# Two side banks and a ring of five, in place of one and six, in the sixteen-head context attentions

## The chip, the core and the metric

One core of a Trainium2 chip runs the kernel. Its engines work side by side: TensorE (PE in the profile, with PEld for its weight loads), VectorE (DVE), ScalarE (ACT), GpSimd (POOL), and the queue that issues transfers (SP). TensorE writes its results into PSUM, which the kernel holds as one tensor `PS` of 8 banks of 512 float32 numbers per partition; DVE and ACT read them from there. The metric is the device time of the kernel in microseconds (us): a median over runs.

## The reference, cut to what matters

The model is twelve sublayers on x, each added to x. Two of them, number 4 (`L1_xattn`) and number 10 (`L3_xattn`), are the ones that the change touches: cross attentions of 64 queries on 1601 context rows, in each of 16 batches, with 16 heads of 16.

```
def _L1_xattn_ref(q, k, v, Wq, bq, Wk, bk, Wv, bv, Wo, bo):   # q: (16, 64, 256); k = v = context: (16, 1601, 128)
    qh = (q @ Wq + bq).reshape(B, LQ, 16, 16).transpose(0, 2, 1, 3)
    kh = (k @ Wk + bk).reshape(B, LKV, 16, 16).transpose(0, 2, 1, 3)
    vh = (v @ Wv + bv).reshape(B, LKV, 16, 16).transpose(0, 2, 1, 3)
    scores = einsum('bhqd,bhkd->bhqk', qh, kh) / sqrt(16)
    attn = softmax(scores, axis=-1)
    out = einsum('bhqk,bhkd->bhqd', attn, vh)
    return out.transpose(0, 2, 1, 3).reshape(B, LQ, 256) @ Wo + bo
...
x = x + _L1_xattn_ref(_layernorm(x), ctx_512, ctx_512, ...)
...
x = x + _L3_xattn_ref(_layernorm(x), ctx_512, ...)            # the same without biases
```

## The kernel before, in words

`perceiver` runs the twelve sublayers one behind the other. `small_xattn` is the body of numbers 4 and 10: it normalizes x, makes the queries, and calls `head_attention` (L2037), the only function that changes. Number 4 (first = True) reads the context by rows, turns it with TensorE and stores the turned form; number 10 loads the turned form. Below they are the first and the second attention.

A batch has 13 tiles of up to 128 context rows (the last has 65). `head_attention` goes by cycles t. Batch and part of a cycle are t divided by 7 and its remainder, j, since a batch takes turns = 7 cycles of two key tiles (one in the last). 16 batches make t = 0 to 111, and before them stand 13 cycles that only prepare (t = -13 to -1). In cycle t TensorE does, in this order (L2292 to L2310):

- ST, `scores_turned(t)`, L2243 and L2252: scores with the keys on the partitions, shifted by the row maximum, into four banks of the ring (one for each group of heads);
- V, `values(t + 10)`, L2216: values of two key tiles, into the side bank;
- W, `weighted(t - 1, 0)`, L2272: half of the product of exps and values, into bank 7;
- S, `scores(t)`, L2231: scores with the queries on the partitions, of cycle t + 8's keys, into the next four banks of the ring, for the maximum alone;
- K, `keys(t + 12)`, L2206: turned keys, into the side bank;
- W, `weighted(t - 1, 1)`, L2272: the other half;
- at the end of a batch's j = 6 the turned row maximum (`max_turned`, L2282), at j = 5 the spread of the row sums (`sums_spread`, L2288), and in the first attention alone C, `context(t + 13)` (L2196), for four cycles of seven (j = 1 to 4; that of j = 4 has 65 columns); all three into the side bank.

Some parts are short: ST at j = 6, V at j = 3, S at j = 5, K at j = 1, and at j = 0 there is one W.

The other engines take these banks in the same order of cycles. ACT: the four exps of ST (`exps`, L2321), the keys (L2330), the sums, the context (L2349). DVE: the values (L2397, with a bias L2400), the four maxima of S (`block_max`, L2372), and once a batch the row maximum and the shift of it (`minus_max`, L2385), for which the next batch's ST waits.

What sets the order is this fixed list, with semaphores. Each fill of the ring has a number; it goes to the bank of that number modulo `banks`, and `wait_fill` lets TensorE wait until the fill with the number `banks` lower has been taken. Both ST and S call `wait_fill` for all four of their banks ahead of their first matmul. ST(t) has the numbers 8t + 32 to 8t + 35, S(t) 8t + 36 to 8t + 39 (for t from 0 to 103). Fills of the side bank are numbered too, and `wait_side` waits until the fill before has been taken.

Of the kernel before, what the change touches and what calls it, by code (L numbers as in the profile page):

```python
# [30 lines left out]
ACT = mybir.ActivationFunctionType  # L31
AX_X = mybir.AxisListType.X

P = 128
# [2002 lines left out]
def head_attention(core, room, Q, made, wv, biased, wo, wo_rows, oT, scale):  # L2037
# [21 lines left out]
    s_lead, v_lead, k_lead, c_lead = 8, 10, 12, 13  # L2059
    first, wk, pair_sel, sum_spread = room.first, made.wk, made.pair_sel, made.sum_spread  # L2060
    context_fills = -(-KT // 4)
    ring, banks, side, out_bank = 3, 6, 6, 7
    st_ready, exp_done = core.semaphore("scores_turned_ready"), core.semaphore("exps_ready")
    s_ready, max_done = core.semaphore("scores_ready"), core.semaphore("block_max_ready")
    top_ready, m_ready = core.semaphore("max_ready"), core.semaphore("shift_ready")
# [33 lines left out]
    for t in cycles:  # L2099
        due = []  # L2100
        if unit(t + v_lead) is not None:
            due.append(("values", t + v_lead))
        if unit(t + k_lead) is not None:
            due.append(("keys", t + k_lead))
        if (b := at_batch(t, turn_at)) is not None:
            due.append(("turn", b))
        if (b := at_batch(t, spread_at)) is not None:
            due.append(("spread", b))
        if (n := context_part(t)) is not None:
            due.append(("context", n))  # L2110
        for fill in due:
            fill_no[fill] = len(taken_by)
            count, by = (dve_no, side_dve) if fill[0] in ("values", "turn") else (act_no, side_act)
            count[fill] = len(count)
            taken_by.append((by, count[fill]))

    def st_fill(t):
        return 4 * (min(t + s_lead, total) + t)
# [16 lines left out]
    with ExitStack() as own:  # L2135
# [11 lines left out]
        with nc.Block() as block:  # L2147
# [29 lines left out]
            def _(pe):  # L2177
                def wait_side(fill):
                    n = fill_no[fill]
                    if n:  # L2180
                        by, count = taken_by[n - 1]
                        pe.wait_ge(by.sem, by.at(count + 1))

                def wait_context(b, to):
# [5 lines left out]
                def context(n):  # L2190
                    b, j = divmod(n, turns)
                    pe.wait_ge(room.landed[b % 2].sem, room.landed[b % 2].at(room.per_batch * (b // 2 + 1)))
                    wait_side(("context", n))
                    for k in range(4 * j, min(4 * j + 4, KT)):
                        kk = keys_of[k]
                        last = nc.tensor.transpose(PS[:, side, (k - 4 * j) * P:(k - 4 * j) * P + kk], room.rows[b % 2][0:kk, k, :],  # L2196
                                                   core.ident[0:kk, 0:kk])
                    last.then_inc(side_ready.sem, 1)

                def keys(t):  # L2200
                    b, u = divmod(t, turns)
                    lo, cols, chunks = key_cuts(u)
                    wait_context(b, lo)
                    wait_side(("keys", t))
                    for n, c in enumerate(chunks):
                        last = nc.tensor.matmul(PS[:, side, n * cols:(n + 1) * cols], wk[:, c * P:(c + 1) * P],  # L2206
                                                room.y[b % 2][:, lo:lo + cols], start=True, stop=True)
                    last.then_inc(side_ready.sem, 1)

                def values(t):  # L2210
                    b, j = divmod(t, turns)
                    wait_context(b, 256 * j)
                    wait_side(("values", t))
                    for n, kt in enumerate(tiles_of(j)):
                        kk = keys_of[kt]
                        last = nc.tensor.matmul(PS[0:kk, side, n * DIM:(n + 1) * DIM], room.y[b % 2][:, kt * P:kt * P + kk], wv[:],  # L2216
                                                start=True, stop=True)
                    last.then_inc(side_ready.sem, 1)

# [59 lines left out]
                def max_turned(b):  # L2279
                    pe.wait_ge(top_ready.sem, top_ready.at(b + 1))  # L2280
                    wait_side(("turn", b))
                    nc.tensor.transpose(PS[:, side, 0:P], M[:].rearrange("p i s -> p (i s)"),  # L2282
                                        core.ident[:]).then_inc(side_ready.sem, 1)

                def sums_spread(b):
                    pe.wait_ge(o_taken.sem, o_taken.at(b + 1))
                    wait_side(("spread", b))
                    nc.tensor.matmul(PS[:, side, 0:4 * SEQ], sum_spread[:], O[:, b % 2, :], start=True,  # L2288
                                     stop=True).then_inc(side_ready.sem, 1)

                pe.wait_ge(filled.sem, filled.at(4))
# [20 lines left out]
            @block.scalar  # L2312
            def _(act):
                def exps(t):
                    b, j = divmod(t, turns)
                    many, kk = len(tiles_of(j)), keys_of[2 * j]
                    if t >= ring:
                        act.wait_ge(av_done.sem, av_done.at(t - ring + 1))
                    act.wait_ge(st_ready.sem, st_ready.at(t + 1))
                    for i in range(groups):  # L2320
                        nc.scalar.activation(probs[0:kk, t % ring, i, 0:many].rearrange("p k c s -> p (k c s)"),  # L2321
                                             PS[0:kk, (st_fill(t) + i) % banks, 0:many * 2 * P], ACT.Exp,
                                             scale=scale).then_inc(exp_done.sem, 1)

                def keys_out(t):
                    b, u = divmod(t, turns)
                    lo, cols, chunks = key_cuts(u)
                    act.wait_ge(side_ready.sem, side_ready.at(fill_no["keys", t] + 1))
                    for n, c in enumerate(chunks):
                        last = nc.scalar.activation(kT[:, b % 2, c, lo:lo + cols], PS[:, side, n * cols:(n + 1) * cols], ACT.Identity)  # L2330
                    last.then_inc(side_act.sem, 1)

                def weighted_out(b):
                    act.wait_ge(av_done.sem, av_done.at((b + 1) * turns))
                    if b >= 2:
                        act.wait_ge(norm_done.sem, norm_done.at(b - 1))
                    nc.scalar.copy(O[:, b % 2, :], PS[:, out_bank, 0:4 * SEQ]).then_inc(o_taken.sem, 1)

                def sums_out(b):
                    act.wait_ge(side_ready.sem, side_ready.at(fill_no["spread", b] + 1))  # L2340
                    nc.scalar.copy(inverse[:, b % 2, :], PS[:, side, 0:4 * SEQ]).then_inc(side_act.sem, 1)

                def context_out(n):
                    b, j = divmod(n, turns)
                    cols = min(512, KEYS - 512 * j)
                    if j == 0 and b >= 2:
                        act.wait_ge(stored[b % 2].sem, stored[b % 2].at(16 * (b // 2)))
                    act.wait_ge(side_ready.sem, side_ready.at(fill_no["context", n] + 1))
                    nc.scalar.copy(room.y[b % 2][:, 512 * j:512 * j + cols], PS[:, side, 0:cols]).then_inc(side_act.sem, 1)  # L2349

                nc.scalar.activation(warm[:], core.ident[0:1, 0:1], ACT.Exp)
                for t in cycles:
                    if unit(t) is not None:
                        exps(t)
                    if unit(t + k_lead) is not None:
                        keys_out(t + k_lead)
                    if (b := at_batch(t, spread_at)) is not None:
                        sums_out(b)
                    if (n := context_part(t)) is not None:
                        context_out(n)  # L2360
                    if (b := at_batch(t, out_at)) is not None:
                        weighted_out(b)

            @block.vector
            def _(dve):
# [16 lines left out]
                def shift_rows(b):  # L2382
                    dve.wait_ge(side_ready.sem, side_ready.at(fill_no["turn", b] + 1))
                    for c in range(DC):
                        last = nc.vector.tensor_scalar(shift[:, b % 2, c, :], PS[:, side, 0:P], pair_sel[:, c:c + 1], None,  # L2385
                                                       ALU.mult).then_inc(m_ready.sem, 1)
                    dve.wait_ge(m_ready.sem, m_ready.at(2 * b + 2))
                    dve.sem_inc(side_dve.sem, 1)

                def values_out(t):  # L2390
                    b, j = divmod(t, turns)
                    kk, many = keys_of[2 * j], len(tiles_of(j))
                    dve.wait_ge(side_ready.sem, side_ready.at(fill_no["values", t] + 1))
                    bank = PS[0:kk, side, 0:many * DIM].rearrange("p (k h d) -> p k h d", h=heads, d=d)
                    out = V[0:kk, b % 2, 2 * j:2 * j + many, :, 0:d]
                    if not biased:
                        ins = nc.vector.tensor_copy(out, bank)  # L2397
# [736 lines left out]
```

## Time and profile before

| what | us |
|---|---|
| median of 3 runs (lowest to highest) | 5926.73 (5922.83 to 5929.96) |
| span of the profiled execution | 5928.5 |
| TensorE busy in the span | 5020.8 (85%) |
| DVE, ACT, GpSimd busy | 3277.9, 2125.8, 954.6 |
| first attention: first C to the first ST, first ST to that of t = 98 | 2032.7 to 2095.3, 2095.3 to 2698.6 |
| second attention: first K to the first ST | 4770.9 to 4821.7 |

The page gives no other time for the profiled execution than its span, which lies inside the range of the three runs; so spans are used as times. A row of the timeline is one group of like instructions in a row on one engine: its start, how long it lasted, and in brackets how long the engine sat idle before it, and whom it waited for. Starts of two groups subtracted give what a cycle costs; busy time alone does not, since pipelined matmuls overlap at their ends by about 0.07 us.

### The profile page before, as it was taken

How to read it: one execution, taken by the hardware profiler on the slowest of the kernel's cores; microseconds unless marked ns; L12 is line 12 of the kernel's file. 1: busy time of each engine (PE TensorE's matmuls, PEld its weight loads, DVE VectorE, ACT ScalarE, POOL GpSimd, SP SyncE). 2: the span in 40 equal slices, each digit the busy share in tenths (PEclk: the TensorE clock that was granted, in tenths of full speed). 3: DMA queues.
4: the chain of work that ended last, by engine and by line, in shares of the span. 5: the costliest groups of instructions: out<-in, count | busy, mean ns of one | idle time of the engine just before them, and what ended most of it. 6: DMA issues, size and time to landing. Idle time of an engine off the chain costs nothing. (4 is left out here: it accounts for less than half of the span.)

```text
span 5928.5 us, 114734 instructions
## 1 busy us (share of the span) xinstructions
PE 5020.8 (85%) x45710; PEld 3724.4 (63%) x45710; DVE 3277.9 (55%) x5626; ACT 2125.8 (36%) x3979; POOL 954.6 (16%) x423
## 2 busy tenths in 40 slices
PE   6879999987599899997756899986579989997877
PEld 4658888874489655555212788875159945555465
DVE  5367777762644455554699433354943355554453
ACT  1245555541155344443221333242024434443121
POOL 0022222100012000000365122142512200000200
PEclk8889999998599899999766899998779989999885
DMA  1010000001111111110010111033311010000020
GB/s 56 27 34 21 14 21 14 14 18 32 38 50 50 29 46 36 45 32 26 36 45 33 65 42 42 21 83 68 92 43 43 28 35 19 25 25 31 29 66 29
DMA packets 193278, 222.86 MB, mean 38 GB/s; under 512 B 44787, under 2 KB 166468, under 8 KB 184676
## 3 DMA queue, kind: packets, MB, share of 16 engines
q1 hardware_dynamic: 188772, 208.54, 11.3%
q10 hardware_dynamic: 4096, 8.40, 0.6%
q8 instruction: 313, 5.13, 0.4%
q14 instruction: 97, 0.79, 0.0%
HBM read 170.09 MB, written 15.34 MB: 31 GB/s over the span
## 5 line engine op out<-in xcount | busy, mean ns | idle before, releaser
L2372 DVE TENSOR_REDUCE block_max<-PS 128x1 f32<-128x512 f32 (+1 forms) x896 | 505.7, 628 | 203.6 <-PE PS L2231 203.6
L1632 PE MATMUL PS<-input_part,part_up 128*128 128x512 f32 x2304 | 552.1, 392 | 18.4 <-DVEq L1713 8.6
L1645 PEld LDWEIGHTS PS<-part_down,hidden_part 128*128 128x128 f32 x4608 | 548.6, 188 | 2.1
L1645 PE MATMUL PS<-part_down,hidden_part 128*128 128x256 f32 x4608 | 549.1, 281 | 0.0
L2321 ACT ACTIVATE probs_turned<-PS 128x512 f32<-128x512 f32 (+1 forms) x896 | 435.0, 571 | 314.6 <-PE PS L2252 314.6
L1632 PEld LDWEIGHTS PS<-input_part,part_up 128*128 128x128 f32 x2304 | 434.3, 189 | 110.3 <-DVEq L1713 9.3
L1685 ACT ACTIVATE hidden<-PS,b 128x512 f32<-128x512 f32 x384 | 265.0, 690 | 650.6 <-PE PS L1632 636.1
L844 PE MATMUL PS<-context_turned,queries 128*128 128x512 f32 x1728 | 411.9, 382 | 25.2 <-issue 18.5
L876 PE MATMUL PS<-probs_turned,context_part 128*128 128x256 f32 (+2 forms) x3120 | 409.2, 286 | 3.7 <-DVE weighted L953 3.7
L1721 DVE TENSOR_TENSOR hidden_part<-hidden,hidden_part 128x512 fp32r<-128x512 f32 x384 | 293.8, 774 | 182.9 <-ACT hidden_part L1675 182.1
L905 ACT CAST probs_turned<-PS 128x512 fp32r<-128x512 f32 x576 | 261.9, 511 | 358.6 <-PE PS L856 358.6
L876 PEld LDWEIGHTS PS<-probs_turned,context_part 128*128 128x128 f32 (+1 forms) x3120 | 382.7, 191 | 4.4 <-DVE probs_turned L919 4.3
L2630 POOL TENSOR_TENSOR fresh<-zT,b_all 128x1024 f32<-128x1024 f32 x64 | 214.4, 3350 | 988.7 <-DMA c_all<-bc_turned 850.7
L919 DVE TENSOR_TENSOR probs_turned<-PS,probs_turned 128x512 fp32r<-128x512 f32 x576 | 311.0, 582 | 97.4 <-ACT probs_turned L905 95.5
L844 PEld LDWEIGHTS PS<-context_turned,queries 128*128 128x128 f32 x1728 | 311.0, 196 | 85.7 <-issue 21.9
L2663 PE MATMUL PS<-prod,ident 128*128 128x512 f32 x256 | 208.4, 961 | 150.4 <-DVE prod L2649 150.4
L2272 PEld LDWEIGHTS PS<-probs_turned,values 128*17 128x17 f32 x13312 | 194.8, 97 | 189.6 <-issue 185.5
L911 ACT ACTIVATE probs<-PS,minus_max 128x1024 f32<-128x1024 f32 (+1 forms) x288 | 268.7, 935 | 87.6 <-DVE minus_max L964 86.7
L1552 POOL TENSOR_TENSOR part_up<-raw_up,part_up 128x2048 fp32r<-128x2048 f32 x24 | 110.4, 4600 | 1176.2 <-ACT part_up L1669 646.2
L1745 DVE SCALAR_TENSOR_TENSOR acc<-PS,gates,acc 128x256 f32<-128x256 f32 x192 | 92.2, 484 | 368.5 <-PE PS L1645 368.5
L959 DVE TENSOR_REDUCE row_max<-PS 128x1 f32<-128x1024 f32 (+1 forms) x288 | 272.7, 982 | 41.8 <-PE PS L844 41.3
L2644 DVE TENSOR_TENSOR_SCAN state<-decay,fresh 128x1024 f32<-128x1024 f32 x64 | 281.4, 4396 | 8.8 <-POOL fresh L2630 8.8
(427 smaller groups left out, 8391.6 us busy)
## 6 DMA issues: line engine op xcount, KB each, us to landing
context_rows<-in_ctx SPq DMA_DIRECT2D x40, 768.0 KB
raw_up<-in_L_ffn_W SPq DMA_DIRECT2D x16, 1024.0 KB, 4.8
raw_down<-in_L_ffn_W SPq DMA_DIRECT2D x16, 1024.0 KB, 4.8
ctx_turned<-context_turned SPq DMA_DIRECT2D x16, 800.5 KB, 4.8
context_turned<-ctx_turned SPq DMA_DIRECT2D x16, 800.5 KB
b_all<-bc_turned SPq DMA_DIRECT2D x16, 512.0 KB, 3.6
c_all<-bc_turned SPq DMA_DIRECT2D x16, 512.0 KB, 4.7
raw_up<-in_L_ffn_wg_w SPq DMA_DIRECT2D x8, 1024.0 KB, 4.8
```

Of the source, the lines that this page charges most:

```text
L844: last = nc.tensor.matmul(S[:, 512 * j:512 * j + cols], qs[a][:, v, p * P:(p + 1) * P], yT[b][:, v, 512 * j:512 * j + cols], start=(m == 0 ...
L876: last = nc.tensor.matmul(O_ps, yp[a][0:kk, u, k, :], probsT[b][0:kk, par, k, :], start=(k == 0 and m == 0), stop=(k == KT - 1 and m == 2))
L911: nc.scalar.activation(probs[:, local % 2, cols], S[:, cols], ACT.Exp, bias=bias[:, local % 2:local % 2 + 1], scale=scale, accum_out=total ...
L919: nc.vector.tensor_tensor(rest, bank, lead, ALU.subtract).then_inc(t_dve.sem, 1)
L959: nc.vector.tensor_reduce(top[:, q, half:half + 1], S[:, cols], AX_X, ALU.max).then_inc(step.sem, 1)
L1632: last = nc.tensor.matmul(PS[:, k % ring + 2 * x, :], bank.parts[name][a][:, c, f * P:(f + 1) * P], h[b][:, c, half * 512:(half + 1) * 512 ...
L1645: last = nc.tensor.matmul(PS[:, 4 + t % outs, 0:DIM], aT[a][:, f, t * P:(t + 1) * P], bank.parts["down"][b][:, f, :], start=(f == 0 and m ...
L1685: nc.scalar.activation(a32[:, k % depth, :], PS[:, k % ring, :], func, bias=b1s[:, bass.ds(e, 1), k % FC:k % FC + 1].squeeze(1)).then_inc( ...
L1721: nc.vector.tensor_tensor(hidden_part(1, k), a32[:, k % depth, :], hidden_part(0, k), ALU.subtract).then_inc(a_split.sem, 1)
L2321: nc.scalar.activation(probs[0:kk, t % ring, i, 0:many].rearrange("p k c s -> p (k c s)"), PS[0:kk, (st_fill(t) + i) % banks, 0:many * 2 * ...
L2372: nc.vector.tensor_reduce(part[:, b % 2, chunks[0]:chunks[-1] + 1, i, u // 2], bank, AX_X, ALU.max).then_inc(max_done.sem, 1)
L2644: nc.vector.tensor_tensor_scan(state[:, c % 2, :], decay[:, c % 2, :], fresh[:, c % 2, :], 0.0, ALU.mult, ALU.add).then_inc(h_ready.sem, 1)
```

## The change

`banks` goes from 6 to 5, and the single side bank (6) becomes two, banks 5 and 6, that the side fills take in turn. `wait_side` waits for the side fill two back instead of one back. `wait_fill` is unchanged in its text, but as `banks` is 5 it now waits for the fill five back. No instruction is added, removed or moved on any engine.

```
-    ring, banks, side, out_bank = 3, 6, 6, 7
+    ring, banks, sides, out_bank = 3, 5, 2, 7
...
+    def side_of(fill):
+        return PS[:, banks + fill_no[fill] % sides, :]
...
                 def wait_side(fill):
                     n = fill_no[fill]
-                    if n:
-                        by, count = taken_by[n - 1]
+                    if n >= sides:
+                        by, count = taken_by[n - sides]
                         pe.wait_ge(by.sem, by.at(count + 1))
...
-                        last = nc.tensor.matmul(PS[:, side, n * cols:(n + 1) * cols], wk[:, c * P:(c + 1) * P],
+                        last = nc.tensor.matmul(side_of(("keys", t))[:, n * cols:(n + 1) * cols], wk[:, c * P:(c + 1) * P],
                                                 room.y[b % 2][:, lo:lo + cols], start=True, stop=True)
...
-                    nc.tensor.transpose(PS[:, side, 0:P], M[:].rearrange("p i s -> p (i s)"),
+                    nc.tensor.transpose(side_of(("turn", b))[:, 0:P], M[:].rearrange("p i s -> p (i s)"),
...
-                    bank = PS[0:kk, side, 0:many * DIM].rearrange("p (k h d) -> p k h d", h=heads, d=d)
+                    bank = side_of(("values", t))[0:kk, 0:many * DIM].rearrange("p (k h d) -> p k h d", h=heads, d=d)
...
```

The lines left out put `side_of` in place of `PS[:, side, ...]` in the same way where the context, the values and the sums are written, and where ACT and DVE read them.

## Rows read from the trace of the kernel before

**Rows 1.** Timeline, TensorE, one batch of the second attention (start, us, engine, line)
```profile
5120.90 1.14 PE L2231 MATMUL PS<-keys_turned,queries 32*128 32x512 f32 x8
...
5123.60 0.50 PE L2243 MATMUL PS<-minus_max,ones_wide 32*128 32x512 f32 x4
...
5126.36 1.14 PE L2231 MATMUL PS<-keys_turned,queries 32*128 32x512 f32 x8 [0.22 <-ACT probs_turned L2321]
...
5137.68 0.67 PE L2231 MATMUL PS<-keys_turned,queries 32*128 32x65 f32 x16
...
5140.18 0.67 PE L2288 MATMUL PS<-weighted,sum_spread 128*128 128x256 f32 x2 [0.21 <-ACT keys_turned L2330]
5140.78 0.39 PE L2243 MATMUL PS<-minus_max,ones_wide 32*128 32x256 f32 x4
...
5147.44 0.50 PE L2243 MATMUL PS<-minus_max,ones_wide 32*128 32x512 f32 x4 [0.99 <-DVE minus_max L2385]
...
5150.40 1.14 PE L2231 MATMUL PS<-keys_turned,queries 32*128 32x512 f32 x8
...
5153.04 0.51 PE L2243 MATMUL PS<-minus_max,ones_wide 32*128 32x512 f32 x4 [0.45 <-DVE block_max L2372]
```

**Rows 2.** Line L2243: who its idle TensorE waited for (us, times)
```profile
  DVE block_max L2372: 24.4, 52
```

**Rows 3.** Timeline, DVE and ACT, the maxima and exps of one cycle
```profile
5151.60 1.29 DVE L2372 TENSOR_REDUCE block_max<-PS 128x1 f32<-128x512 f32 x2 [0.98 <-PE PS L2231]
...
5151.60 2.48 DVE L2372 TENSOR_REDUCE block_max<-PS 128x1 f32<-128x512 f32 x4 [0.98 <-PE PS L2231]
...
5154.56 1.09 ACT L2321 ACTIVATE probs_turned<-PS 128x512 f32<-128x512 f32 x2 [1.07 <-PE PS L2252]
...
5154.56 2.07 ACT L2321 ACTIVATE probs_turned<-PS 128x512 f32<-128x512 f32 x4 [1.07 <-PE PS L2252]
```

**Rows 4.** Timeline, TensorE, cycles with C in the first attention
```profile
2319.29 1.14 PE L2231 MATMUL PS<-keys_turned,queries 32*128 32x512 f32 x8
...
2322.11 0.51 PE L2243 MATMUL PS<-minus_max,ones_wide 32*128 32x512 f32 x4
...
2325.07 1.14 PE L2231 MATMUL PS<-keys_turned,queries 32*128 32x512 f32 x8
...
2328.04 0.63 PE L2196 MATMUL PS<-ident,context_rows 128*128 128x128 f32 x4 [0.21 <-ACT keys_turned L2330]
2328.60 0.51 PE L2243 MATMUL PS<-minus_max,ones_wide 32*128 32x512 f32 x4
...
2337.86 1.14 PE L2231 MATMUL PS<-keys_turned,queries 32*128 32x512 f32 x8
...
2341.07 0.50 PE L2243 MATMUL PS<-minus_max,ones_wide 32*128 32x512 f32 x4
```

**Rows 5.** Timeline, TensorE, the head of either attention
```profile
2067.51 1.14 PE L2231 MATMUL PS<-keys_turned,queries 32*128 32x512 f32 x8
...
2091.01 1.14 PE L2231 MATMUL PS<-keys_turned,queries 32*128 32x512 f32 x8
...
4773.18 2.04 PE L2206 MATMUL PS<-context_turned,wk 128*128 128x512 f32 x2 [0.78 <-ACT keys_turned L2330]
...
4798.71 1.14 PE L2231 MATMUL PS<-keys_turned,queries 32*128 32x512 f32 x8
...
4817.44 1.14 PE L2231 MATMUL PS<-keys_turned,queries 32*128 32x512 f32 x8
```

**Rows 6.** Timeline, TensorE, the tail of the first attention
```profile
2698.56 0.50 PE L2243 MATMUL PS<-minus_max,ones_wide 32*128 32x512 f32 x4 [0.98 <-DVE minus_max L2385]
...
2726.40 0.51 PE L2243 MATMUL PS<-minus_max,ones_wide 32*128 32x512 f32 x4 [0.92 <-DVE block_max L2372]
...
2739.76 0.51 PE L2243 MATMUL PS<-minus_max,ones_wide 32*128 32x512 f32 x4 [0.34 <-ACT probs_turned L2321]
```

**Rows 7.** Stretches: us, busy us of PE, PEld, DVE, ACT, POOL, PEclk, DMA
```profile
2094.00:2098.00 4.00, 3.01 (x38) 2.51 (x39) 1.22 (x4) 0.34 (x1) 0.00 (x0) 0.69 0.00 0
...
2725.00:2730.00 5.00, 3.30 (x134) 2.81 (x130) 2.57 (x5) 2.07 (x4) 0.00 (x0) 1.00 0.02 3
...
5120.00:5280.00 160.00, 150.69 (x2985) 90.77 (x2987) 90.78 (x157) 71.80 (x151) 0.00 (x0) 1.00 0.07 23
```

More of the change, by code:

```diff
@@ L2195, in context @@
                         kk = keys_of[k]
-                        last = nc.tensor.transpose(PS[:, side, (k - 4 * j) * P:(k - 4 * j) * P + kk], room.rows[b % 2][0:kk, k, :],
+                        last = nc.tensor.transpose(side_of(("context", n))[:, (k - 4 * j) * P:(k - 4 * j) * P + kk], room.rows[b % 2][0:kk, k, :],
                                                    core.ident[0:kk, 0:kk])
@@ L2215, in values @@
                         kk = keys_of[kt]
-                        last = nc.tensor.matmul(PS[0:kk, side, n * DIM:(n + 1) * DIM], room.y[b % 2][:, kt * P:kt * P + kk], wv[:],
+                        last = nc.tensor.matmul(side_of(("values", t))[0:kk, n * DIM:(n + 1) * DIM], room.y[b % 2][:, kt * P:kt * P + kk], wv[:],
                                                 start=True, stop=True)
@@ L2287, in sums_spread @@
                     wait_side(("spread", b))
-                    nc.tensor.matmul(PS[:, side, 0:4 * SEQ], sum_spread[:], O[:, b % 2, :], start=True,
+                    nc.tensor.matmul(side_of(("spread", b))[:, 0:4 * SEQ], sum_spread[:], O[:, b % 2, :], start=True,
                                      stop=True).then_inc(side_ready.sem, 1)
@@ L2329, in keys_out @@
                     for n, c in enumerate(chunks):
-                        last = nc.scalar.activation(kT[:, b % 2, c, lo:lo + cols], PS[:, side, n * cols:(n + 1) * cols], ACT.Identity)
+                        last = nc.scalar.activation(kT[:, b % 2, c, lo:lo + cols], side_of(("keys", t))[:, n * cols:(n + 1) * cols], ACT.Identity)
                     last.then_inc(side_act.sem, 1)
@@ L2340, in sums_out @@
                     act.wait_ge(side_ready.sem, side_ready.at(fill_no["spread", b] + 1))
-                    nc.scalar.copy(inverse[:, b % 2, :], PS[:, side, 0:4 * SEQ]).then_inc(side_act.sem, 1)
+                    nc.scalar.copy(inverse[:, b % 2, :], side_of(("spread", b))[:, 0:4 * SEQ]).then_inc(side_act.sem, 1)
                 def context_out(n):
@@ L2348, in context_out @@
                     act.wait_ge(side_ready.sem, side_ready.at(fill_no["context", n] + 1))
-                    nc.scalar.copy(room.y[b % 2][:, 512 * j:512 * j + cols], PS[:, side, 0:cols]).then_inc(side_act.sem, 1)
+                    nc.scalar.copy(room.y[b % 2][:, 512 * j:512 * j + cols], side_of(("context", n))[:, 0:cols]).then_inc(side_act.sem, 1)
                 nc.scalar.activation(warm[:], core.ident[0:1, 0:1], ACT.Exp)
@@ L2384, in shift_rows @@
                     for c in range(DC):
-                        last = nc.vector.tensor_scalar(shift[:, b % 2, c, :], PS[:, side, 0:P], pair_sel[:, c:c + 1], None,
+                        last = nc.vector.tensor_scalar(shift[:, b % 2, c, :], side_of(("turn", b))[:, 0:P], pair_sel[:, c:c + 1], None,
                                                        ALU.mult).then_inc(m_ready.sem, 1)
```

## The prediction

> **What bounds the kernel now.** I first read the stretches, to see which engine sets the pace where the change acts. In the second attention TensorE is busy 150.69 of 160 us at a granted clock of 1.00 (2.4 GHz), DVE 90.78 and ACT 71.80 [rows 7]. So TensorE nearly sets the pace, with some 6% idle. Then I read TensorE's own timeline over one batch, for what ends that idle time. There are four kinds of wait: for the maxima (0.45 us at 5153.04), for the exps (0.22 us at 5126.36), for `minus_max` at the start of each batch (0.99 us at 5147.44), and for the single side bank (0.21 us at 5140.18, behind the keys) [rows 1]. The first two are waits of the ring, the last is the wait that the change is about. Line L2243 waits for the maxima 52 times, 24.4 us in all [rows 2]: the ring of six is already just too small in those cycles, and just large enough in the others.
>
> The two time spans that decide are from one ST to the S behind it, and from that S to the next ST.
>
> **What a ring of five waits for.** ST(t) begins at number F = 8t + 32. With six banks its four fills wait for F-6 to F-3: the last exps of ST(t-1), and the first two maxima of S(t-1). With five they wait for F-5 to F-2: one exp and the first three maxima. In the same way S(t) waits today for the last two maxima of S(t-1) and the first two exps of ST(t); with five banks for the first three exps. All waits stand ahead of the first matmul. So each ST waits for one maximum more, each S for one exp more.
>
> One maximum more is (2.48 - 1.29)/2 = 0.60 us later, one exp more (2.07 - 1.09)/2 = 0.49 us later [rows 3].
>
> Where the ring is the limit today the spans can be read: S to ST by the maxima takes 5153.04 - 5150.40 = 2.64, ST to S by the exps 5126.36 - 5123.60 = 2.76 [rows 1]. With the change these bounds become 2.64 + 0.60 = 3.24 and 2.76 + 0.49 = 3.25, and nothing that TensorE has to do in between is that long, except with C. One cycle then lasts 6.49 us. These are rows of this kernel with one step of this kernel added, so I take them at their value. Below them the cost could be nothing, if the engines were ahead of TensorE by a maximum; the waits of 0.45 and 0.22 exclude that. Above them, a wake-up could be paid once more: 0.15 us lie between the end of the second maximum (5151.60 + 1.29) and ST at 5153.04 [rows 1, 3], and 0.15 at some 12 waits a batch in 28 batches is 50 us more, 6066. I take the value without it, since that 0.15 is already inside 2.64 and 2.76.
>
> **The second attention, batch by batch.** ST to S: 2.96 where V is whole (5150.40 - 5147.44 [rows 1]; j = 0, 1, 2, 4, 5), becomes 3.25: five times +0.29. At j = 3 (V short) +0.49. At j = 6 ST is short, its exps are done in time: no change. Together +1.94. S to ST: +0.60 at j = 0 and j = 1, where the maxima decide already. At j = 2, 3, 4 it is 2.70 (5123.60 - 5120.90 [rows 1]) and becomes 3.24: three times +0.54. At j = 5 S is short and its maxima are no limit; the wait of the sums' spread for the keys goes, 0.21 and the 0.05 of overlap that a wait costs, -0.26. At j = 6 the next ST waits for `minus_max`, which stands on DVE behind all four maxima: what is gained for the turned maximum is hidden by them, no change. Together 1.20 + 1.62 - 0.26 = +2.56. A batch costs +4.50. For t = 0 to 97, 14 batches: **+63.0 us**.
>
> **The first attention.** ST to S as before, +1.94. S to ST holds C at j = 1 to 4. At j = 1 it is 2.82 (2322.11 - 2319.29) and becomes 3.24, +0.42. At j = 2 and 3 it is 3.53 (2328.60 - 2325.07), of which 0.26 is C's wait for the keys [rows 4]; that goes, 3.27 is left, and the maxima's 3.24 lie below it: twice -0.26. At j = 4 3.21 (2341.07 - 2337.86 [rows 4]) becomes 3.24, +0.03. At j = 0 +0.60, at j = 5 -0.26. Together +0.27, a batch +2.21. 14 batches: **+30.9 us**. Here the change gets some of its gain, and C's work covers part of the new wait.
>
> **The tails.** From t = 98 on no C and soon no K is left. The five cycles from 2698.56 to 2726.40 take 27.84 [rows 6] and become 5 x 6.49 = 32.45: +4.6. Then one exp step +0.5, and five cycles in which ST alone waits for the exps (0.34 us at 2739.76 [rows 6]), each +0.49: +2.4. Two tails of +7.5: **+15.0 us**.
>
> **The heads.** In the cycles without ST the side bank is the limit: V waits for the keys, K for the values, at 0.78 us each (as at 4773.18 [rows 5]). This goes, and the maxima's bound takes its place where S runs: S to S 3.24. Second attention: the five cycles from 4798.71 to 4817.44 take 18.73 [rows 5]; four of them become 3.27, the one behind the short S 2.8 (V, S and K by TensorE's own time), 15.9: -2.8. Before 4798.71, six fills run at 1.2 GHz one behind the other instead of with 0.78 to 0.88 us between them; if the clock rises at the same moment as today, that leaves -4.3. First attention: from 2067.51 to 2091.01 23.50 [rows 5] becomes 16.5 (C, V, S and K without waits: 3.3, 3.3, 3.8, 3.4, 2.8): -7.0, and before it -5.1. Together **-19.2 us**. An earlier rise of the clock would give up to 5 us more in each head; a fall of it at the end of the head, as at 2094 [rows 7], costs some 2 us now and may or may not come.
>
> **The sum**: 63.0 + 30.9 + 15.0 - 19.2 = +89.7 on a span of 5928.5, 6018. The span lies 1.8 us above the median, so the forecast is 5926.7 + 89.7 = **6016 us**, 1.5% slower.
>
> The Trainium skill ("Perfetto Trace Analysis", Optimization Strategy) says that the same gap repeating on the engine that should be saturated can mean too little PSUM for the next tile. By it the gaps at C, the spread and the turned maximum speak for a second side bank, but those at L2243 speak for the ring, which is larger in count; the trace agrees with the rule for both.
>
> **Rivals.**
>
> A. The gain of the side banks shows and the ring has slack enough (faster). Its place: all waits for the side bank, its price the heads' -19.2, -0.26 for three cycles of a first-attention batch and one of a second, 14 x 1.04 = -14.6; together -34, 5893 us. It decides if a third maximum is taken by the time that ST comes. Against it: at 5153.04 ST waits already for the second [rows 1].
>
> B. The clock. With 6.49 us cycles TensorE has some 0.8 us idle in each, in two pieces. At 2094 the granted clock fell to 0.69 for 4 us, after a head with gaps in each cycle [rows 7]. If it fell like that at each of 32 batch starts, at 2 us each, the time would be 64 us more, 6080. Against it: from 2725 to 2730 TensorE is busy 3.30 of 5 us, with longer gaps than the change makes, at clock 1.00 [rows 7]. The Trainium skill ("TensorE: Matmul & The Clock Gate", A second HAM failure mode: psum-queue depth-cycling) describes just this, small idle times between groups that cycle through banks making the clock swing. By the rule rival B would hold; no row of the main loop shows it.
>
> C. The new waits cost less than I count, half of 0.29 and 0.54, because TensorE's own groups could slip behind one another or maxima start earlier: 93.9 + 15.0 halved, minus 19.2, is +35, 5962 us. For it nothing speaks but that small waits have hidden slack; against it, that both bounds are read from waits.
>
> D. The ring and the side banks balance, within 0.2% (12 us, about what a measurement of this kernel can tell from no change): it needs a third of the ring's cost and all of the heads' gain.
>
> **Chances.** The forecast, from 5995 to 6040: 0.78. B 0.07. C 0.07. D 0.03. A 0.04; 0.01 for the rest. The range that holds the time 8 times in 10 reaches down for the heads' clock and part of C and up for the wake-ups: 5988 to 6045. Slower 0.93, same 0.03, faster 0.04.
>
> **What would show it.** Right: on L2243 the waits for the maxima grow from 24.4 us to above 100 us, and stand in front of nearly every ST of the second attention; on L2231 waits for the exps appear in six cycles of seven, about 0.3 us each; a batch of the second attention lasts 45.2 us instead of 40.7, one of the first 45.3 instead of 43.1; L2196, L2282, L2288, L2216 and L2206 wait for no keys or values. The first ST stands about 12 us and 7 us earlier behind the start of its attention. Wrong: batches as long as today, or a granted clock below 1.00 between the batches.

## The result and the profile after

The changed kernel takes 5996.46 us (median of four runs, 5994.20 to 6003.85), the kernel before 5924.79 us beside it (5922.83 to 5929.96). The ratio is 1.0121, with a 95% interval from 1.0107 to 1.0136: slower by 71.7 us where 89.7 were forecast. The forecast was 6016 us with a range from 5988 to 6045; the result lies inside it, 19.5 us below the forecast. The profiled span grew from 5928.5 to 5994.3 us, by 65.8; the account below is one of the spans.

The code stands three lines further down in the changed kernel: ST is L2246 and L2255, S L2234, V L2219, K L2209, C L2199, W L2275, the turned maximum L2285, the maxima L2375, the exps L2324.

First the page of the changed kernel. DVE and ACT do what they did; what changed is when TensorE may write.

```profile
PE 5013.0 (84%) x45710; PEld 3726.0 (62%) x45710; DVE 3276.2 (55%) x5626; ACT 2123.5 (35%) x3979; POOL 955.5 (16%) x423
```

The same 160 us of the second attention as in [rows 7], with the same columns, and who line L2246 waited for (us, times), as in [rows 2]:

```profile
5120.00:5280.00 160.00, 137.64 (x2698) 83.67 (x2694) 83.38 (x145) 64.46 (x136) 0.00 (x0) 1.00 0.06 18
```
```profile
  DVE minus_max L2388: 88.6, 64
  DVE block_max L2375: 82.9, 122
  ACT probs_turned L2324: 9.5, 12
```

TensorE is busy 137.64 of 160 us instead of 150.69, still at a granted clock of 1.00. Both attentions together, ST's waits for the maxima rose from 24.4 us in 52 cases to 82.9 in 122, and S (L2234) waits for the exps 57.6 us in 177 cases. Which instruction waits, and how long the cycle becomes, is seen in TensorE's timeline of one batch (start, us, engine, line, with the idle time ahead and its releaser in brackets). It answers to [rows 1]:

```profile
5180.10 0.50 PE L2246 MATMUL PS<-minus_max,ones_wide 32*128 32x512 f32 x4 [1.24 <-DVE minus_max L2388]
...
5183.35 1.14 PE L2234 MATMUL PS<-keys_turned,queries 32*128 32x512 f32 x8 [0.23 <-ACT probs_turned L2324]
...
5186.59 0.50 PE L2246 MATMUL PS<-minus_max,ones_wide 32*128 32x512 f32 x4 [1.04 <-DVE block_max L2375]
...
5189.83 1.14 PE L2234 MATMUL PS<-keys_turned,queries 32*128 32x512 f32 x8 [0.22 <-ACT probs_turned L2324]
...
5199.53 0.51 PE L2246 MATMUL PS<-minus_max,ones_wide 32*128 32x512 f32 x4 [0.46 <-DVE block_max L2375]
...
5202.76 1.14 PE L2234 MATMUL PS<-keys_turned,queries 32*128 32x512 f32 x8 [0.68 <-ACT probs_turned L2324]
...
5206.00 0.51 PE L2246 MATMUL PS<-minus_max,ones_wide 32*128 32x512 f32 x4 [0.47 <-DVE block_max L2375]
```

ST to S is 5183.35 - 5180.10 = 3.25, S to ST 5186.59 - 5183.35 = 3.24: the two bounds of the forecast, to the hundredth. In the second attention 75 of the 112 STs wait for the maxima and 16 more for `minus_max`; S waits in six cycles of seven in both. In the first attention a cycle with C answers to [rows 4]:

```profile
2315.99 1.14 PE L2234 MATMUL PS<-keys_turned,queries 32*128 32x512 f32 x8 [0.70 <-ACT probs_turned L2324]
...
2318.68 0.66 PE L2199 MATMUL PS<-ident,context_rows 128*128 128x128 f32 x4
2319.27 0.51 PE L2246 MATMUL PS<-minus_max,ones_wide 32*128 32x512 f32 x4
```

C waits for no keys any more, and S to ST is 3.28 instead of 3.53: here the side bank's gain shows.

From TensorE's timeline I took four marks in each attention: the first side fill (C or K), the first ST, ST(98), the last ST. What lies between the first two is called the head below, what lies between the first and the last ST the loop, and what lies between ST(98) and the last ST the tail. For the changed kernel these are the ST marks of the first attention and then of the second:

```profile
2067.12 0.51 PE L2246 MATMUL PS<-minus_max,ones_wide 32*128 32x512 f32 x4 [1.96 <-DVE minus_max L2388]
...
2700.71 0.51 PE L2246 MATMUL PS<-minus_max,ones_wide 32*128 32x512 f32 x4 [1.24 <-DVE minus_max L2388]
```
```profile
4819.23 0.50 PE L2246 MATMUL PS<-minus_max,ones_wide 32*128 32x512 f32 x4 [1.96 <-DVE minus_max L2388]
...
5450.77 0.50 PE L2246 MATMUL PS<-minus_max,ones_wide 32*128 32x512 f32 x4 [1.24 <-DVE minus_max L2388]
```

The main loop of 14 batches lasts 633.59 and 631.54 us, before 603.28 and 570.04. With the same marks in every kernel that ran (us, of one profiled execution each; the tail is part of the loop; the last column runs from the last spread of the row sums to the end of the program):

| kernel | span | head 1 | loop 1 | head 2 | loop 2 | behind the second |
|---|---|---|---|---|---|---|
| before | 5928.5 | 62.6 | 656.9 | 50.8 | 623.9 | 478.3 |
| after | 5994.3 | 40.1 | 694.0 | 34.3 | 691.7 | 478.5 |
| e1, ring 5, side 1 | 6034.6 | 62.6 | 704.5 | 50.8 | 694.9 | 466.2 |
| e2, ring 4, sides 3 | 6189.0 | 40.1 | 790.3 | 37.7 | 788.4 | 477.9 |
| e3, ring 6, side 2 in the head | 5873.4 | 39.7 | 655.6 | 32.9 | 622.2 | 460.0 |
| e4, before, TensorE kept busy in the head | 5908.0 | 54.7 | 656.3 | 44.6 | 623.0 | 479.1 |
| e5, after, waits by group | 5938.6 | 40.2 | 675.5 | 33.9 | 669.8 | 460.0 |
| e6, e3 and waits by group | 5879.5 | 40.1 | 649.7 | 32.9 | 615.4 | 478.2 |
| e7, e3 and a later wait at the start | 5880.4 | 39.1 | 655.5 | 31.5 | 622.0 | 477.1 |
| e8, e3, e6 and e7 together | 5862.0 | 41.0 | 651.9 | 31.6 | 616.7 | 466.1 |

The heads and loops repeat within about two microseconds where the code is the same. Other stretches, which no edit touches, do not. The last column takes 460 to 479 us. Its length goes with its mean granted clock: 0.75 in the six kernels that take 477 to 479 us, 0.78 in the two that take 466, 0.79 and 0.80 in the two that take 460. The other engines do the same work in the same time (the kernel before, then e5, columns as in [rows 7]):

```profile
5450.20:5928.50 478.30, 374.68 (x2050) 252.31 (x2048) 221.06 (x378) 80.00 (x135) 40.55 (x32) 0.75 0.15 47
```
```profile
5478.60:5938.60 460.00, 354.42 (x2050) 239.30 (x2048) 221.07 (x378) 79.87 (x135) 40.46 (x32) 0.80 0.16 49
```

The first C stands between 2022.4 us (e4) and 2036.2 us (e5) behind the start, and the stretch from the last ST of the first attention to the first K of the second takes 2018.8 (before, e1) to 2024.5 us (e6). So differences of under some 20 us between two kernels are read from the heads and loops, not from the spans.

### The profile page after: what moved, and what is told of

The parts are those of the page before. It is cut to its first block and busy times, and to the rows that moved or that the text cites. A ratio compares the mean times of both kernels' runs of the same rounds, so it can differ in the third digit from the quotient of the medians.

```text
span 5994.3 us, 114734 instructions
## 1 busy us (share of the span) xinstructions
PE 5013.0 (84%) x45710; PEld 3726.0 (62%) x45710; DVE 3276.2 (55%) x5626; ACT 2123.5 (35%) x3979; POOL 955.5 (16%) x423
## 5 line engine op out<-in xcount | busy, mean ns | idle before, releaser
L2375 DVE TENSOR_REDUCE block_max<-PS 128x1 f32<-128x512 f32 (+1 forms) x896 | 505.4, 627 | 259.4 <-PE PS L2234 258.9
L2324 ACT ACTIVATE probs_turned<-PS 128x512 f32<-128x512 f32 (+1 forms) x896 | 434.7, 570 | 382.6 <-PE PS L2255 382.6
L2275 PEld LDWEIGHTS PS<-probs_turned,values 128*17 128x17 f32 x13312 | 194.5, 97 | 187.8 <-issue 183.7
L2234 PE MATMUL PS<-keys_turned,queries 32*128 32x512 f32 (+1 forms) x2048 | 241.1, 549 | 60.1 <-ACT probs_turned L2324 57.6
```

What stands on the lines that cost most here:

```text
L2375: nc.vector.tensor_reduce(part[:, b % 2, chunks[0]:chunks[-1] + 1, i, u // 2], bank, AX_X, ALU.max).then_inc(max_done.sem, 1)
```

## The experiments

**e1: the ring alone.** Five banks for the ring and one side bank; bank 6 stays unused.

```diff
-    ring, banks, sides, out_bank = 3, 5, 2, 7
+    ring, banks, sides, out_bank = 3, 5, 1, 7
```

> The ring of five alone: five banks for scores, one side bank, bank 6 unused. Theory (one evacuation more is waited for by every ST and every S): the main loops cost what they cost in the changed kernel, and what the second side bank gives is missing. A batch of the second attention lasts 45.1 + 0.26 = 45.4 us, one of the first 45.26 + 0.79 = 46.0 us (against 40.7 and 43.1 before); the heads are as before, 62.5 and 50.8 us to the first ST. In all 14 x 2.9 + 14 x 4.7 + 13 for the tails = +120 over before, 6045 us, slower than the changed kernel by 48. Rival (the two side banks that alternate are what slows the main loops, the ring is not): batches of 40.7 and 43.1 us, 5925 us.

Measured: 6043.79 us (6045 expected), ratio 1.0192 [1.0175, 1.021]. The loops grow by 47.6 and 71.0 us, the heads do not move at all. The rival, that the two alternating side banks are what slows the loops, falls, as here there is one. So having five banks in the ring in place of six costs 118.6 us in the loops. The second side bank gives back 10.5 and 3.2 us in the loops (704.5 to 694.0, 694.9 to 691.7) and all of the heads' gain; the prediction has 0.26 us for this in three cycles of a first-attention batch and in one of a second-attention batch, which in 14 batches is 10.9 and 3.6. In the first attention C waits for the keys as before, and S for the exps of the smaller ring:

```profile
2305.46 0.63 PE L2199 MATMUL PS<-ident,context_rows 128*128 128x128 f32 x4 [0.21 <-ACT keys_turned L2333]
...
2309.27 1.14 PE L2234 MATMUL PS<-keys_turned,queries 32*128 32x512 f32 x8 [0.22 <-ACT probs_turned L2324]
```

**e2: one bank further.** Four ring banks, three side banks: if one bank costs a maximum and an exp per cycle, the next one costs the same again.

```diff
-    ring, banks, sides, out_bank = 3, 5, 2, 7
+    ring, banks, sides, out_bank = 3, 4, 3, 7
```

> Twice the dose: four banks for scores, three side banks in turn. Theory: each ST waits for the fourth maximum of the S before it, each S for the fourth exp: S to ST 2.64 + 2 x 0.60 = 3.84 us, ST to S 2.76 + 2 x 0.49 = 3.74 us. A batch of either attention lasts 6 x 3.74 + 2.39 + 5 x 3.84 + 2.83 + 4.26 = 51.1 us (45.1 and 45.3 in the changed kernel); in all 14 x 6.0 + 14 x 5.9 + 17 for the tails + 5 for the heads = 188 us more than the changed kernel, about 6184 us. Rival (the cost of the change is one for having a wait at all, not for each bank): as the changed kernel, about 5996 us, or a step much smaller than the first.

Measured: 6192.07 us (6184 expected), ratio 1.0438 [1.042, 1.0455], loops 96.3 and 96.7 us above those of the changed kernel, where the expectation adds up to 92 each. The timeline gives 5307.13 - 5303.30 = 3.83 from S to ST and 3.73 from ST to S, where 3.84 and 3.74 were expected:

```profile
5303.30 1.14 PE L2234 MATMUL PS<-keys_turned,queries 32*128 32x512 f32 x8 [1.18 <-ACT probs_turned L2324]
...
5307.13 0.50 PE L2246 MATMUL PS<-minus_max,ones_wide 32*128 32x512 f32 x4 [1.06 <-DVE block_max L2375]
...
5310.86 1.14 PE L2234 MATMUL PS<-keys_turned,queries 32*128 32x512 f32 x8 [0.70 <-ACT probs_turned L2324]
```

So one bank less again costs one maximum and one exp per cycle. It shows in full here, while in the step from six to five a part was hidden where the ring of six had not been the limit. The rival, one price for having a wait at all, falls. Some of the 4 us more than expected go with short falls of the clock. Besides one near the first ST each loop of e2 shows two between the first batch and ST(98), of under 4 us each, and the second loop has a longer one in its tail (near 5670 us). The changed kernel's loops show none but the one at the first ST of the second attention. This is rival B's mechanism, but only at the double dose:

```profile
5336.00:5340.00 4.00, 4.00 (x70) 3.01 (x64) 0.38 (x1) 2.07 (x4) 0.00 (x0) 0.58 0.00 0
```

The Trainium skill ("TensorE: Matmul & The Clock Gate", A second HAM failure mode: psum-queue depth-cycling) says that small idle times between groups that cycle through banks can make the clock swing. With the ring of five the trace does not agree (clock 1.00 over 160 us with TensorE busy 137.64); with four it shows such a fall. That the short waits caused it is not shown.

**e4: the clock's share of the heads.** The kernel before, with three transposes into an unused part of the out bank behind each side fill of the cycles before the first S, and behind the keys of one cycle more. The waits for the single side bank all stay, but in the early part of the head TensorE's gaps are partly filled (0.28 to 0.55 us in place of 0.78 to 0.88).

```diff
+                def keep_warm(many):
+                    for _ in range(many):
+                        nc.tensor.transpose(PS[:, out_bank, 256:256 + P], core.ident[:], core.ident[:])
...
+                        keep_warm(3 if t < -s_lead else 0)
```

> The kernel before, with three 128 x 128 transposes of the identity into an unused part of bank 7 behind each side fill of the cycles before the first S (and behind the first keys after it), that is, into TensorE's idle time there; its waits stay. It asks what the clock alone is worth in the heads. Theory (the clock rises earlier in the changed kernel because TensorE has less idle time): the granted clock reaches 1.00 some 5 us into either head instead of 29 and 21 us; fills take about 1.1 in place of 2.05 us, and the waits of 0.78 us stay: -9 and -6, 5910 us. Rival (the rise does not depend on TensorE's idle time in the head): the clock rises when it does before, 5925 us or a few us more for the transposes.

Measured: 5906.95 us (5910 expected), ratio 0.9953 [0.9936, 0.9969]; the heads shorten by 7.9 and 6.2 us (9 and 6 expected), the loops stay. The rest of the spans' 20.5 us lies where no edit is: the first C stands 10.3 us earlier in e4, and the stretch between the attentions is 5.0 us longer. The stretches below give clock and busy time at the start of the first head: the kernel before (28 us of it), then e4, then the changed kernel.

```profile
2034.00:2062.00 28.00, 20.72 (x39) 8.15 (x39) 4.19 (x7) 4.08 (x9) 0.00 (x0) 0.51 0.24 65
```
```profile
2022.00:2026.00 4.00, 3.51 (x9) 2.09 (x10) 0.00 (x0) 0.58 (x1) 0.31 (x1) 0.50 0.25 66
2026.00:2030.00 4.00, 3.42 (x16) 2.05 (x14) 0.00 (x0) 1.42 (x3) 0.00 (x0) 0.82 0.01 4
```
```profile
2028.00:2032.00 4.00, 3.71 (x8) 1.94 (x9) 0.00 (x0) 1.42 (x3) 0.00 (x0) 0.57 0.26 57
2032.00:2036.00 4.00, 3.16 (x13) 1.65 (x11) 0.69 (x1) 1.78 (x4) 0.00 (x0) 1.00 0.00 0
```

Before, TensorE stays at its lower level (1.2 GHz, 0.51) in these 28 us, in which it is busy for 20.72, with waits of 0.78 to 0.88 us between the fills. With the gaps filled in part (e4: mean 0.82 from 2026 to 2030, the first C at 2022.4) or gone (the changed kernel: 1.00 from 2032, the first C at 2027.0) the clock rises some 5 us behind the first fill. So of the changed kernel's -39.0 us in the heads some 14.1 come by the clock, which leaves 24.9 for the waits. That the two add up, and that the transposes cost nothing themselves, is assumed, not shown.

**e3: both.** The ring keeps six banks. The bank of the outputs is idle in the head, so it serves as second side bank until the first turned maximum, and is cleared behind the last side fill in it.

```diff
-    ring, banks, sides, out_bank = 3, 5, 2, 7
+    ring, banks, out_bank = 3, 6, 7
...
+    def side_bank(n):
+        return banks + n % 2 if n < head_fills else banks
...
+                    if t == 0:
+                        by, count = taken_by[last_odd]
+                        if by is side_act:
+                            dve.wait_ge(by.sem, by.at(count + 1))
+                        nc.vector.memset(PS[:, out_bank, 0:4 * SEQ], 0.0).then_inc(out_cleared.sem, 1)
```

> The second side bank without the smaller ring: six banks for scores throughout; the side fills before the first turned maximum alternate between bank 6 and bank 7, which nothing else uses until then (its clearing is moved behind them), and all later ones go to bank 6 as before. Theory: batches as before (43.1 and 40.7 us), tails as before, heads as in the changed kernel (40.1 and 34.4 us to the first ST against 62.5 and 50.8): 5925 - 39 = 5886 us. Rival (only the waits that go are worth something, the earlier rise of the clock in the changed kernel was another thing): -19 us, 5906 us. A second rival (a head gains and gives it back at the first batches): 5925 us.

Measured: 5873.51 us (5886 expected), ratio 0.9908 [0.9887, 0.9929]. Heads -22.9 and -17.9 (-39 expected in all), loops -1.3 and -1.7 against the kernel before, 43.8 us in all. Both rivals fall: the gain is more than that of the waits alone, and the loops do not give it back. The loops' -1.3 and -1.7 are no gain of the edit: in the kernel before the clock falls right behind each first ST (0.54 from 2095.3 to 2099.0, below), and in e3 it does not. The timed difference of 58 has some of the chance in the last stretch (460.0 instead of 478.3) in it. In the head S follows S at 2050.79 - 2047.80 = 2.99 with no wait in between, where the ring of five has 3.23 (4799.52 - 4796.29) with a wait; first e3, then the changed kernel:

```profile
2047.80 1.14 PE L2242 MATMUL PS<-keys_turned,queries 32*128 32x512 f32 x8
...
2050.79 1.14 PE L2242 MATMUL PS<-keys_turned,queries 32*128 32x512 f32 x8
```
```profile
4796.29 1.14 PE L2234 MATMUL PS<-keys_turned,queries 32*128 32x512 f32 x8 [0.18 <-DVE block_max L2375]
...
4799.52 1.14 PE L2234 MATMUL PS<-keys_turned,queries 32*128 32x512 f32 x8 [0.17 <-DVE block_max L2375]
```

And ST waits for the maxima exactly as in [rows 2]:

```profile
  DVE block_max L2385: 24.4, 52
```

**e5: the waits taken one by one.** In the changed kernel all four waits of ST and of S stand ahead of the first matmul. Here each group waits only for its own bank. The edit in S, with the same in ST:

```diff
-                    for i in range(groups):
-                        wait_fill(pe, s_fill(t) + i)
...
+                            if n == 0:
+                                wait_fill(pe, s_fill(t) + i)
```

> The changed kernel with its ring waits taken apart: TensorE waits for the bank of a group of heads just ahead of that group's first matmul, not for all four ahead of the first. Theory (the last of the four banks is on the chain, whichever matmul waits for it): the four groups of S start within 0.1 us of one another and run side by side, so the wait of the fourth holds S's end back as before; only the first three bias matmuls of ST slip in front of theirs. A batch stays at 45 us, or falls by at most 5 x 0.3 = 1.5 us for ST: 5975 to 5996 us. Rival (the cost is made by standing all four waits in front; the groups whose banks are free could run in the time lost): batches of 42.1 and 41.1 us, about 5890 us, faster than the kernel before.

Measured: 5945.29 us (ten runs), ratio 1.0032 [1.0018, 1.0046]. The loops shorten by 18.5 and 21.9 us against the changed kernel. From the first ST to ST(98) it is 16.2 and 19.6 us, 1.2 and 1.4 a batch, so the bound of 1.5 per batch held. The expected total of 5975 to 5996 us was missed: 28 batches of 1.5 are 42 us, which leaves 5954 and not 5975, and the last stretch takes 460.0 us here instead of 478.5. The rival (the place of the waits is what the ring costs, 5890) falls: a batch still lasts 44.1 and 43.7 us, where the rival wanted 42.1 and 41.1. One batch, ST to ST, is 43.71 us:

```profile
5159.97 1.49 PE L2245 MATMUL PS<-minus_max,ones_wide 32*128 32x512 f32 x4
...
5203.68 1.48 PE L2245 MATMUL PS<-minus_max,ones_wide 32*128 32x512 f32 x4
```

ST's first row is 1.49 long here instead of 0.51: its four groups start one after another as their banks come free. So the place of the waits is 40 us of the ring's 118.6 in the loops; the rest stays.

**e6, e7, e8: what can be added to e3.** e6 splits the waits as e5 does; e7 moves TensorE's wait for GpSimd's clearings from the start of each attention to t = 0 (the edit below is against e3); e8 is both.

```diff
-                pe.wait_ge(filled.sem, filled.at(3))
...
+                    if t == 0:
+                        pe.wait_ge(filled.sem, filled.at(3))
```

> The same taking apart of the ring waits, in the kernel with six banks for scores and the second side bank in the head alone. Theory: less than 0.4 us a batch to gain on the 52 waits for maxima and the waits for exps, 14 x 2 batches, and twice as many wait positions: ratio to before 0.988 to 0.992 (without: 0.9908). Rival as above: a batch loses its waits, 1.0 us each, ratio 0.985 or less.

> Six banks for scores, the second side bank in the head alone, and TensorE no longer waits for GpSimd's four clearings ahead of its first side fill: that wait goes to the first ST, where it has long been met (DVE takes one of it ahead of the first row maximum). Theory: TensorE stands idle 4.0 us in front of the first fill and then runs its first fills at 1.2 GHz; the wait is worth about 3 us in each attention, and 2 to 3 us more if the shorter idle time leaves the clock at 2.4 GHz: heads of 38 and 31 us counted from the first fill, and that fill 2.5 to 3 us earlier behind the queries; -6 to -12 us, ratio to before 0.989. Rival (the first fill waits for something else as well, the block's start or the context's transfer): no change against the kernel without it.

> All three together: six banks for scores, the second side bank in the head alone, ring waits taken apart, and the wait for GpSimd's clearings moved to the first ST. Theory: by the profiles of the parts, against the kernel before: heads -41 (22.9 + 17.9), their later wait -4 in front and -2 inside, first to last ST -13 (of 655.6 and 622.2 without the split waits to 649.7 and 615.4): about -60 on 5929, ratio 0.990, 5869 us; the gain of -5.9 and -6.8 from the split waits should be seen again between first and last ST. Rival (the parts hide one another, or what was seen in the parts was chance of the rest of the program): ratio above 0.992, and first to last ST again 655 and 622 us.

Measured: e6 5875.24 us, ratio 0.9903 [0.987, 0.9936]; e7 5870.07, 0.9899 [0.9872, 0.9927]; e8 5865.93, 0.9896 [0.988, 0.9913]. By the marks e6's loops are 5.9 and 6.8 us shorter than e3's; from the first ST to ST(98) it is 4.1 and 4.5 us, 0.3 a batch, below the 0.4 that was expected. e7's heads are 0.6 and 1.4 us shorter than e3's. The idle time ahead of e7's first C is 1.98 us where e3 has 4.00, so the first fill comes 2.0 us earlier and not 2.5 to 3; the 6 to 12 us that were expected in all are not shown by times that differ by 3.4 us:

```profile
2035.75 0.66 PE L2207 MATMUL PS<-ident,context_rows 128*128 128x128 f32 x4 [4.00 <-POOL values L2184]
```
```profile
2030.37 0.63 PE L2207 MATMUL PS<-ident,context_rows 128*128 128x128 f32 x4 [1.98 <-PEq L1951]
```

e8 was to be 60 us faster than the kernel before and is 62.5. Its loops are 3.7 and 5.5 us shorter than e3's, where 5.9 and 6.8 were expected, and its first head is 1.9 us longer than e7's, though the code of the head differs only in the place of the waits. There the granted clocks differ (e7's first head, then e8's and the first us behind its first ST; us, PE busy, PEclk, DMA share, GB/s):

```profile
2030.40:2069.50 39.10, 33.03 (x163) 1.00 0.34 91
```
```profile
2029.30:2070.30 41.00, 35.79 (x163) 0.92 0.32 87
2070.30:2074.00 3.70, 3.66 (x39) 0.54 0.00 0
```

So one or two microseconds of a head or a loop can be the clock of that execution. In total the four versions with the ring of six cannot be told apart, as their intervals overlap. All four beat the kernel before; e8 has the lowest median, 1.0% below it.

## Why the prediction was right, and where it was off

**The ring's bounds held.** 3.24 and 3.25 were forecast and measured, and e2 gave the same step once more. e1, where only the ring is smaller, has the whole price, and rivals A and D fall with it: the ring had not the slack that they need.

**The batches.** Second attention 631.54 / 14 = 45.11 us (forecast 45.2), first 633.59 / 14 = 45.26 (45.3): +61.5 and +30.3 us, forecast +63.0 and +30.9. Rival C wanted half.

**The tails.** Forecast +15.0, measured 694.0 + 691.7 - 633.59 - 631.54 less the same of before (656.9 + 623.9 - 603.28 - 570.04), which is +13.1. The five cycles of [rows 6] and the exp step came out (+5.3 in each attention, for 4.6 + 0.5), and so did the five cycles in which ST alone waits for the exps (+2.4 and +2.3, for 2.4). The last cycle became shorter instead, 3.24 us in both attentions where it was 4.12 and 4.57: in the kernel before an idle time of about 1 us within W stands there, which is gone. I did not find what it waited for.

**The heads: the mis-sized term.** The forecast took -19.2 for both and measured are 62.6 - 40.1 = 22.5 and 50.8 - 34.3 = 16.5, together -39.0. The step that failed is "if the clock rises at the same moment as today". I had read that TensorE runs at 1.2 GHz there, but not asked what held the clock down. The heads can be split at the third S, as in the prediction (2067.51 and 4798.71 in [rows 5]). From the first side fill to the third S, before, changed and e4 (us, PE busy, PEclk, DMA share, GB/s):

```profile
2032.70:2067.50 34.80, 25.64 (x61) 0.61 0.20 55
...
4770.90:4798.70 27.80, 21.33 (x48) 0.63 0.04 9
```
```profile
2027.00:2045.50 18.50, 16.59 (x61) 0.91 0.38 102
...
4784.90:4799.50 14.60, 14.27 (x48) 0.88 0.07 17
```
```profile
2022.40:2049.30 26.90, 22.01 (x96) 0.91 0.26 70
...
4757.20:4778.80 21.60, 17.93 (x69) 0.92 0.05 12
```

And the five cycles from the third S on, in the changed kernel:

```profile
2045.51 1.14 PE L2234 MATMUL PS<-keys_turned,queries 32*128 32x512 f32 x8 [0.17 <-DVE block_max L2375]
...
2062.86 1.14 PE L2234 MATMUL PS<-keys_turned,queries 32*128 32x512 f32 x8
```
```profile
4814.97 1.14 PE L2234 MATMUL PS<-keys_turned,queries 32*128 32x512 f32 x8
```

These five cycles take 17.35 and 15.45 us (4814.97 - 4799.52) instead of 23.50 and 18.73: -9.4, forecast -7.0 and -2.8. So this part of the term was right. The early parts became 29.5 us shorter in all, and the forecast had -5.1 and -4.3 for them. e4 has the clock's gain there with the waits in place, 7.9 + 6.2 = 14.1 us; the prediction allowed 5 in each head and put none into its sum. TensorE's idle time there (length less busy time) fell by 7.3 and 6.1 us, 13.4 in all, which is 4.0 more than the 9.4 priced. I read this as the same wrong step again: with the moment of the rise held fixed, a wait that goes only lets more fills run at the lower clock. These two make 27.5 of the 29.5. The 2.0 that are left stay open. The fall of the clock that the prediction put at the end of the head has no part in this: it begins behind the first ST (2095.3), in the loop.

```profile
2095.30:2099.00 3.70, 3.70 (x40) 0.54 0.00 0
```

In the changed kernel the clock does not fall at the first ST of the first attention, and falls at that of the second (columns as in [rows 7]):

```profile
2068.00:2072.00 4.00, 3.27 (x34) 1.64 (x26) 1.19 (x2) 2.06 (x4) 0.00 (x0) 1.00 0.00 0
...
4820.00:4824.00 4.00, 4.00 (x36) 2.12 (x28) 0.69 (x1) 2.06 (x4) 0.00 (x0) 0.57 0.00 0
```

**The account.** 61.5 + 30.3 + 13.1 - 39.0 = +65.9, against +65.8 in the spans. That it closes to 0.1 is luck: outside the marks the first C stands 5.7 us earlier in the changed kernel, the stretch between the attentions is 5.0 us longer and the last one 0.5, and these cancel. By the marks, the forecast's 89.7 is 19.8 too high by the heads, and 4.0 by loops and tails.

**The signs.** The waits for the maxima were to go above 100 us and came to 82.9, 53.5 of them in the second attention and 29.4 in the first, where C fills part of the time. Cycles were as long as forecast, so the sign was a poor one; the times from ST to S and back were the good one. The waits for the exps came as forecast (177 cases, 0.33 us each), and in the loop the side fills wait for no keys or values. The first STs came 22.5 and 16.5 us earlier behind the first side fills, where about 12 and 7 were forecast.

**Rival B.** Behind the fall at the first ST of the second attention the clock holds at 1.00 in the changed kernel's loops, where the rival wanted a fall at each of 32 batch starts; only e2, with waits of 1.18 and 1.06 us in a cycle, shows short falls there.

## What to carry to other kernels

Where a ring of banks already makes the matmul wait, a bank less costs the spacing of the consumers' instructions (here 0.60 us for a maximum, 0.49 for an exp) in each cycle in which the ring is the limit, so price a change of its size from the timeline's distance of two evacuations. A bank that is wanted only in the fill of a pipeline should be borrowed there from a buffer that is not used yet: e3 takes the side bank's gain and leaves the ring alone. And gaps of under a microsecond cost twice in the early part of these heads, 13.4 us in themselves and 14.1 us in the TensorE clock that did not rise, so put both into the sum.

## What the runs showed of the hardware

- In the first head of the kernel before the granted clock stayed at 0.51 for 28 us, in which TensorE was busy for 20.72 us with waits of 0.78 to 0.88 us between the fills. With the gaps partly filled (e4) or gone (the changed kernel) it rose within about 5 us of the first fill.
- With TensorE busy 137.64 of 160 us, in two waits per cycle, the clock held at 1.00. It fell in e2 to 0.58 for 4 us in which the profile shows TensorE busy for all 4.00, and in the kernel before to 0.54 right behind the first ST (3.70 busy us of 3.70). In e7 it stayed at 1.00 through both heads, in e8 through the second alone.
- The stretch behind the second attention varies from 460 to 479 us between executions of code that is the same there, with a mean granted clock from 0.80 down to 0.75. Why the clock differs is open.
